# A fused transformer block and graph attention: another assignment and order of the steps on the engines

## The reference, cut to what matters

```python
cmod = silu(c) @ w_ada + b_ada            # six parts of 128
x_mod = ln(x) * (1 + scale_msa) + shift_msa
k, q, v = split(x_mod @ w_qkv, 3)
w = softmax((q / 8) @ k^T)                # per sequence and head, 32 x 32
x = x + gate_msa * ((w @ v) @ w_proj + b_proj)
h = gelu((ln(x) * (1 + scale_mlp) + shift_mlp) @ w_mlp1 + b_mlp1)
x = x + gate_mlp * (h @ w_mlp2 + b_mlp2)
# layer 1: v = x, q = c
self = concat(v, where(sum(v) == 0, 0, q)) @ W_self^T + b_self
for d in (0, 1):                          # adj or its transpose, [:, :, :20]
    aff = (self @ Wq[d]^T + bq) @ (self[:, :20] @ Wk[d]^T + bk)^T / sqrt(8)
    aff = where(sum(A) > 0, aff, -9e15) + (A @ w_bias + b_bias)
    output += (softmax(aff) @ self[:, :20]) @ Wout[d] + bout[d]
return v + relu(self + output)
```

## Time and profile before

| | |
|---|---|
| median of 3 runs | 96.94 us (96.56 to 97.03) |
| the profiled execution | 95.63 us, its span 93.8 us |
| TensorE busy | 83.7 us, 89% of the span |
| VectorE busy | 71.7 us, 76% |
| ScalarE busy | 55.7 us, 59% |
| GpSimd busy | 46.1 us, 49% |
| SyncE's DMA queue | 5.31 MB in 3,496 packets |

### The profile page before, as it was taken

How to read it: one execution, slowest core, us unless ns; L and a number is a source line. 1 busy time by engine, 2 the same in 40 slices (tenths; PEclk the granted TensorE clock), 3 DMA queues, 4 the chain that set the end, 5 groups by cost and what they waited for, 6 DMA issues and landing times.

```text
span 93.8 us, 4196 instructions
## 1 busy us (share of the span) xinstructions
PE 83.7 (89%) x1802; PEld 67.5 (72%) x1802; DVE 71.7 (76%) x183; ACT 55.7 (59%) x127; POOL 46.1 (49%) x72
## 2 busy tenths in 40 slices
...
DMA packets 3778, 5.75 MB, mean 61 GB/s; under 512 B 720, under 2 KB 2896, under 8 KB 3632
## 3 DMA queue, kind: packets, MB, share of 16 engines
q1 hardware_dynamic: 3496, 5.31, 20.6%
...
...
## 4 chain that ended last, share of the span: by engine, by line
PE 65%; DVE 15%; issue 6%; POOL 5%; ACTq 4%; ACT 2%; POOLq 0%; DVEq 0%
PE ps_s L1043 8%; PE ps_b L964 8%; PE ps_b L944 7%; PE ps_b L919 6%; PE ps_b L895 5%; PE ps_b L1069 5%; ACTq L752 4%; PE ps_b L1061 4%; PE ps_b L970 4%; PE ps_b L1091 3%; PE ps_b L912 3%; POOL E L676 3%; DVE neg_max L1445 3%; PE ps_b L1100 2%; PE ps_b L952 2%
## 5 line engine op out<-in xcount | busy, mean ns | idle before, releaser
L1227 ACT ACTIVATE PT<-ps_b 120x384 f32<-120x384 f32 x16 | 7.4, 487 | 8.6 <-PE ps_b L1061 4.6
L1141 ACT ACTIVATE hidden<-ps_b,cols 128x256 f32<-128x256 f32 x16 | 7.0, 474 | 6.5 <-PE ps_b L964 6.5
L856 POOL TENSOR_TENSOR rstd<-var_eps,minus_half 128x2 f32<-128x2 f32 (+1 forms) x9 | 6.0, 668 | 6.3 <-DVE var_eps L1261 6.2
L784 POOL TENSOR_TENSOR Kb<-k_raw,head_mask 128x640 f32<-128x640 f32 x4 | 5.0, 1258 | 8.1 <-ACT k_raw L1156 5.4
L1436 DVE TENSOR_TENSOR E<-ps_s,bias_rep 128x640 f32<-128x640 f32 x8 | 6.6, 823 | 3.0 <-PE ps_b L1061 1.7
L964 PE MATMUL ps_b<-xm,w_rest_sb 128*128 128x256 f32 x32 | 8.6, 385 | 0.0
L676 POOL TENSOR_TENSOR E<-E,neg_max 128x640 f32<-128x640 f32 x5 | 6.4, 1271 | 4.4 <-DVE neg_max L1445 3.9
L1043 PE MATMUL ps_s<-Kb,home_b 32*32 32x80 f32 x512 | 7.4, 239 | 0.7 <-DVE E L1436 0.7
L970 PE MATMUL ps_b<-hidden,w_rest_sb 128*128 128x256 f32 x32 | 7.6, 386 | 0.0
L647 POOL TENSOR_TENSOR xm<-xm,cmod 128x256 f32<-128x256 f32 (+1 forms) x6 | 3.5, 586 | 8.3 <-DVE xm L1283 8.3
L1043 PEld LDWEIGHTS ps_s<-Kb,home_b 32*32 32x32 f32 x512 | 5.7, 103 | 2.4 <-issue 1.5
(11 more groups left out here) (120 smaller groups left out, 218.0 us busy)
## 6 DMA issues: line engine op xcount, KB each, us to landing
...
```

Source lines behind the costliest of these rows:

```text
L856: ins = pool.tensor_tensor(rstd[:, layer, g0:g1], var_eps[:, layer, g0:g1], minus_half[:, 0:g1 - g0], ALU.pow)
L1141: return act.activation(hidden[:, slot_of(h), j, 0:n], ps[:, 0:n], ACT.Gelu_apprx_tanh, bias=cols[:, R_MLP1 + j:R_MLP1 + j + 1])
L1227: ins = act.activation(PT[0:KR, key % 3, 0:CH, :], ps[0:KR, 0:CH * P].rearrange("p (j t) -> p j t", t=P), ACT.Exp)
```

## The change

Nothing of the arithmetic changes: the list has the same 480 steps. FILL goes from 14 products of ones to 5. In ON and TAKE_ON 55 steps change their engine. ORDER and BANKS are another permutation and another choice of banks. The parts that the text below speaks of:

- The products of ones: 12 ahead of k 0 and 2 ahead of xnT 2 before; now 2 ahead of the transpose xnT 0, 1 ahead of q 0, 2 ahead of k 2.
- Start: shift 0 goes to GpSimd, the eviction of q 0 and zero vz1a to ScalarE, the spread of k 0 to GpSimd.
- Steps with two SBUF operands change between VectorE and GpSimd (resid1, resid2, shift, sub, ya, yb, spreads of k1).
- Scores of the two units of a group stand next to each other in TensorE's list before. Now other steps stand between scores 14 and 15, 16 and 17, 18 and 19, and 21 and 20, and in layer 0 between 6 and 7.
- Part 1 of V 1's spread of mid 3 moves from ScalarE's queue to SyncE's, behind part 0 and ahead of the first store. The product v1 of mid 3 stands ahead of scores 17 (behind scores 16).
- Layer 1's first scores, 9 and 8, stand behind more products of mids 1 to 3.

```diff
--- before.py
+++ after.py
@@ -62,7 +62,7 @@
 ZERO_K = (0, 0)
 ZERO_V = (0, 0)
 WARM = 5
-FILL = {('k', 0): 12, ('xnT', 2): 2}
+FILL = {('xnT', 0): 2, ('q', 0): 1, ('k', 2): 2}
...
+ ('resid1', 0): 'dve',
  ('resid1', 2): 'dve',
+ ('resid1', 3): 'dve',
  ('resid2', 0): 'dve',
- ('resid2', 3): 'dve',
- ('shift', (0, 0)): 'dve',
+ ('shift', (0, 0)): 'pool',
  ('shift', (1, 0)): 'dve',
- ('shift', (1, 1)): 'dve',
- ('spread', ('k', 0)): 'act',
+ ('shift', (1, 2)): 'dve',
+ ('shift', (1, 3)): 'dve',
+ ('spread', ('k', 0)): 'pool',
  ('spread', ('k', 1)): 'act',
- ('spread', ('k', 2)): 'act',
- ('spread', ('k', 3)): 'pool',
- ('spread', ('k', 4)): 'act',
+ ('spread', ('k', 2)): 'pool',
+ ('spread', ('k', 3)): 'act',
+ ('spread', ('k', 4)): 'pool',
  ('spread', ('k1', 0, 0)): 'dve',
  ('spread', ('k1', 0, 1)): 'pool',
- ('spread', ('k1', 1, 0)): 'act',
- ('spread', ('k1', 1, 1)): 'pool',
- ('spread', ('k1', 2, 0)): 'act',
- ('spread', ('k1', 2, 1)): 'pool',
- ('spread', ('k1', 3, 0)): 'pool',
- ('spread', ('k1', 3, 1)): 'act',
+ ('spread', ('k1', 1, 0)): 'dve',
+ ('spread', ('k1', 1, 1)): 'act',
+ ('spread', ('k1', 2, 0)): 'dve',
+ ('spread', ('k1', 2, 1)): 'act',
+ ('spread', ('k1', 3, 0)): 'act',
+ ('spread', ('k1', 3, 1)): 'dve',
  ('spread', ('v', 0)): 'act',
- ('spread', ('v', 1)): 'pool',
- ('spread', ('v', 2)): 'act',
- ('spread', ('v', 3)): 'act',
- ('spread', ('v', 4)): 'pool',
- ('spread', ('v1', 3, 1)): 'act',
+ ('spread', ('v', 1)): 'act',
+ ('spread', ('v', 2)): 'pool',
+ ('spread', ('v', 3)): 'pool',
+ ('spread', ('v', 4)): 'act',
+ ('spread', ('v1', 3, 1)): 'sp',
  ('sub', 5): 'dve',
- ('sub', 6): 'dve',
- ('sub', 7): 'pool',
+ ('sub', 6): 'pool',
+ ('sub', 7): 'dve',
  ('sub', 8): 'pool',
  ('sub', 9): 'pool',
  ('sub', 10): 'pool',
  ('sub', 11): 'pool',
- ('sub', 12): 'dve',
+ ('sub', 12): 'pool',
+ ('ya', 2): 'dve',
+ ('ya', 3): 'dve',
+ ('ya', 4): 'dve',
  ('ya', 6): 'dve',
  ('ya', 7): 'dve',
- ('yb', 0): 'dve',
- ('yb', 2): 'dve',
+ ('yb', 1): 'dve',
+ ('yb', 5): 'dve',
+ ('yb', 6): 'dve',
  ('yb', 7): 'dve',
+ ('zero', 'vz1a'): 'act',
...
- (('k', 3), 0): 'dve',
- (('k', 4), 0): 'dve',
- (('k1', 0, 0), 0): 'dve',
  (('k1', 0, 1), 0): 'dve',
  (('k1', 1, 0), 0): 'dve',
- (('k1', 2, 0), 0): 'dve',
- (('k1', 2, 1), 0): 'dve',
- (('q', 0), 0): 'dve',
  (('q', 1), 0): 'dve',
- (('q', 3), 0): 'dve',
- (('sbtok', 0), 0): 'dve',
- (('sbtok', 1), 0): 'dve',
- (('x2tok', 1), 0): 'dve',
- (('x2tok', 2), 0): 'dve',
- (('yT', 0), 0): 'dve',
- (('yT', 1), 0): 'dve'}
+ (('q', 2), 0): 'dve',
+ (('q1', 0, 0), 0): 'dve',
+ (('q1', 0, 1), 0): 'dve',
+ (('q1', 1, 0), 0): 'dve',
+ (('q1', 2, 0), 0): 'dve',
+ (('q1', 2, 1), 0): 'dve',
+ (('sbtok', 3), 0): 'dve',
+ (('yT', 2), 0): 'dve'}
...
-ORDER = [('zero', 'v1_ones'), ('consts', 0), ('zero', 'v0_ones'), ('zero', 'pad'), ('ident', 0), ('masks', 0), ('plus1', 0),
- ('zero', 'vz1a'), ('apply', 0), ('dense', ('xnT', 0)), ('take', (('cmod', 0), 0)), ('take', (('xnT', 0), 0)),
- ('zero', 'vz1b'), ('stats', (0, 1)), ('stats', (0, 2)), ('shift', (0, 0)), ('stats', (0, 3)), ('dense', ('k', 0)),
- ('dense', ('q', 0)), ('fetch', 0), ('rstd', (0, 1)), ('dense', ('v', 0)), ('dense', ('cmod', 1)), ('fetch', 2),
- ('rstd', (0, 2)), ('take', (('q', 0), 0)), ('apply', 1), ('fetch', 1), ('take', (('k', 0), 0)),
...
- ('take', (('xn2T', 3), 0)), ('scores', 9), ('take', (('rowsum', 1), 0)), ('scores', 8), ('shift', (1, 3)),
...
- ('exp', 17), ('scores', 20), ('spread', ('v1', 3, 0)), ('spread', ('v1', 3, 1)), ('turn', 16), ('addx', 2),
- ('badd', 11), ('turn', 19), ('ya', 3), ('turn', 18), ('selfb', 3), ('max', 11), ('scores', 22), ('scores', 23),
...
+ORDER = [('zero', 'v0_ones'), ('ident', 0), ('zero', 'v1_ones'), ('masks', 0), ('consts', 0), ('zero', 'pad'), ('silu', 0),
+ ('plus1', 0), ('sel', 0), ('gbias', 0), ('zero', 'vz1a'), ('dense', ('cmod', 0)), ('stats', (0, 0)),
+ ('take', (('cmod', 0), 0)), ('rstd', (0, 0)), ('apply', 0), ('dense', ('xnT', 0)), ('take', (('xnT', 0), 0)),
+ ('stats', (0, 1)), ('shift', (0, 0)), ('zero', 'vz1b'), ('stats', (0, 2)), ('dense', ('q', 0)), ('rstd', (0, 1)),
+ ('dense', ('k', 0)), ('apply', 1), ('dense', ('v', 0)), ('rstd', (0, 2)), ('stats', (0, 4)), ('dense', ('xnT', 1)),
...
+ ('spread', ('k1', 1, 0)), ('dense', ('k1', 2, 1)), ('scores', 9), ('scores', 8), ('take', (('v1', 1, 0), 0)),
...
+ ('scores', 14), ('max', 7), ('values', 10), ('values', 8), ('take', (('self', 3), 0)), ('scores', 15), ('exp', 11),
+ ('sub', 7), ('dense', ('q1', 3, 1)), ('dense', ('k1', 3, 0)), ('badd', 8), ('take', (('q1', 3, 1), 0)),
+ ('values', 9), ('take', (('k1', 3, 0), 0)), ('values', 11), ('recip', 5), ('scores', 16), ('spread', ('k1', 3, 0)),
+ ('spread', ('v1', 2, 0)), ('max', 8), ('turn', 13), ('dense', ('v1', 3, 0)), ('mult', 5), ('sub', 8), ('recip', 6),
+ ('exp', 13), ('scores', 17), ('take', (('v1', 3, 0), 0)), ('dense', ('k1', 3, 1)), ('mult', 6), ('turn', 12),
...
+ ('selfb', 1), ('take', (('sbtok', 0), 0)), ('scores', 18), ('take', (('x2tok', 0), 0)), ('values', 12), ('yb', 1),
+ ('values', 14), ('max', 9), ('yb', 0), ('relu', 1), ('values', 13), ('exp', 15), ('addx', 1), ('scores', 19),
+ ('relu', 0), ('recip', 7), ('sub', 9), ('values', 15), ('badd', 10), ('dense', ('sbtok', 1)),
+ ('spread', ('v1', 3, 0)), ('dense', ('q1', 3, 0)), ('mult', 7), ('take', (('sbtok', 1), 0)), ('addx', 0),
+ ('scores', 21), ('max', 10), ('take', (('q1', 3, 0), 0)), ('turn', 17), ('selfb', 2), ('turn', 16), ('ya', 2),
+ ('exp', 17), ('sub', 10), ('recip', 8), ('dense', ('sbtok', 2)), ('mult', 8), ('exp', 16), ('scores', 20),
+ ('take', (('sbtok', 2), 0)), ('dense', ('x2tok', 2)), ('spread', ('v1', 3, 1)), ('badd', 11),
+ ('dense', ('x2tok', 1)), ('selfb', 3), ('take', (('x2tok', 2), 0)), ('turn', 18), ('take', (('x2tok', 1), 0)),
...
+ ('addx', 2), ('turn', 21), ('recip', 9), ('store', (2, 4)), ('exp', 20), ('sub', 12), ('values', 19), ('mult', 9),
+ ('exp', 21), ('values', 20), ('recip', 10), ('mult', 10), ('values', 21), ('ya', 4), ('turn', 22), ('recip', 11),
+ ('ya', 5), ('turn', 23), ('mult', 11), ('exp', 22), ('yb', 4), ('exp', 23), ('ya', 6), ('values', 22), ('yb', 5),
...
```

More of the change, by code:

```diff
@@ L166 @@
+ (('q1', 1, 0), 0): 'dve',
[3 more added lines that the diff above has]
+ (('yT', 2), 0): 'dve'}
 BANKS = {('cmod', 0): 0,
- ('xnT', 0): 1,
+ ('xnT', 0): 0,
+ ('q', 0): 0,
  ('k', 0): 1,
- ('q', 0): 0,
  ('v', 0): 2,
- ('cmod', 1): 3,
- ('xnT', 1): 0,
+ ('xnT', 1): 3,
  ('xnT', 2): 3,
- ('xnT', 3): 0,
- ('k', 1): 3,
- ('q', 1): 2,
- 'qz': 1,
+ ('cmod', 1): 2,
+ ('k', 1): 1,
+ ('q', 1): 0,
  ('v', 1): 3,
- ('k', 2): 1,
+ ('xnT', 4): 1,
+ 'qz': 3,
+ ('k', 2): 0,
@@ L180 @@
+ ('xnT', 3): 3,
  ('q', 2): 2,
- ('turn', 0): 1,
- ('xnT', 4): 0,
- ('v', 2): 2,
- ('v', 3): 3,
- ('turn', 1): 2,
- ('k', 3): 0,
- ('q', 3): 3,
- ('q', 4): 1,
- ('values', 0): 0,
- ('v', 4): 2,
+ ('turn', 0): 3,
+ ('v', 3): 0,
+ ('k', 3): 1,
+ ('q', 3): 2,
+ ('v', 2): 0,
+ ('values', 0): 2,
+ ('q', 4): 1,
+ ('turn', 1): 0,
+ ('k', 4): 3,
+ ('v', 4): 1,
+ ('yT', 0): 2,
+ ('turn', 3): 1,
  ('turn', 2): 3,
- ('k', 4): 2,
- ('yT', 0): 0,
- ('turn', 3): 0,
- ('proj', 0): 1,
+ ('proj', 0): 2,
  ('values', 1): 3,
- ('bias', 0): 2,
+ ('turn', 5): 2,
@@ L198 @@
  ('x1tok', 0): 1,
  ('turn', 4): 3,
- ('turn', 5): 0,
- ('values', 2): 0,
- ('values', 3): 3,
+ ('bias', 0): 0,
+ ('values', 2): 3,
+ ('values', 3): 2,
  ('xn2T', 0): 1,
- ('turn', 6): 3,
+ ('turn', 7): 3,
+ ('yT', 1): 2,
+ ('turn', 6): 1,
  ('yT', 2): 0,
- ('turn', 7): 1,
- ('yT', 1): 2,
  ('mlp1', 0, 0): 3,
+ ('proj', 1): 2,
  ('proj', 2): 0,
- ('proj', 1): 1,
- ('mlp1', 0, 2): 2,
- ('mlp1', 0, 3): 0,
- ('mlp1', 0, 1): 1,
+ ('mlp1', 0, 2): 1,
+ ('mlp1', 0, 3): 2,
+ ('mlp1', 0, 1): 0,
  ('x1tok', 2): 3,
- ('values', 4): 2,
@@ L216 @@
[L216 to L218 removed]
+ ('values', 4): 1,
+ ('x1tok', 1): 2,
+ ('mlp2', 0): 0,
+ ('yT', 3): 1,
  ('xn2T', 2): 3,
[L220 to L237 removed]
+ ('xn2T', 1): 2,
@@ L238 @@
+ ('proj', 3): 1,
+ ('rowsum', 0): 0,
+ ('self', 0): 3,
+ ('mlp1', 2, 2): 2,
+ ('mlp1', 2, 0): 0,
+ ('mlp1', 1, 2): 1,
+ ('q1', 0, 0): 2,
+ ('k1', 0, 0): 0,
+ ('k1', 0, 1): 3,
+ ('mlp1', 1, 1): 1,
+ ('v1', 0, 0): 2,
+ ('mlp1', 2, 1): 3,
+ ('mlp1', 1, 3): 1,
+ ('x1tok', 3): 0,
+ ('mlp1', 1, 0): 2,
+ ('q1', 0, 1): 3,
  ('mlp1', 2, 3): 1,
- ('v1', 0, 0): 3,
  ('mlp2', 1): 2,
- ('mlp2', 2): 3,
- ('self', 1): 2,
- ('x2tok', 1): 0,
- ('xn2T', 3): 1,
- ('rowsum', 1): 3,
- ('x2tok', 2): 1,
- ('rowsum', 2): 3,
```

269 lines of the change are left out of this document (122 added, 147 removed), and 7 rows, old and new, of the table ORDER.

## The result

The changed kernel took 98.34 us (median of 20 runs, 96.82 to 99.84), the kernel before beside it 96.44 (20 runs, 95.41 to 97.80). The ratio is 1.016, 95% interval 1.012 to 1.021: slower by 1.6%, where 1.8% faster was forecast. The profiled execution took 97.89 (span 96.2) against 95.63 (span 93.8) before.

The account below looks back on a forecast made before the run. TensorE and VectorE were nearly full, leaving about 3 us of holes plus waste at the start and behind the last product. Terms -0.8 -0.2 -0.5 -0.4 +0.4 -0.2 = -1.7 us take the median 96.94 to 95.2; range 93.4 to 97.4.

Parts of the forecast that it names:

- The start: Up to the first subtraction: fewer products of ones let real products start sooner, gaining 0.8 us, bounds 0 and 1.8.
- The term for xnT 0: First transpose at the start: two products of ones ahead of it cost 0.65 us, making it some 0.3 us later.
- The clock: TensorE at the start: 1.2 GHz until activity releases 2.4 GHz; fewer ones leave no long early run to release it.
- rival B: Start: clock stays at 1.2 GHz to about 17, products take 1.7 us more, gain gone, 97.0; chance 0.14.
- beyond 15: Sign at the start: TensorE products at low pace beyond 15 us would show the forecast wrong.
- The middle: From 17 to 56 us: same work in nearly the same order, gain 0.2 us, bounds 0 and 0.6.
- Two-operand steps: Layer 1, VectorE beside GpSimd: keeping these steps apart gains 0.5 of 1.7 us of waiting, bounds 0 and 1.6.
- The last spread: V 1's last spread, moved to SyncE's queue: ends exp 16's wait on issue, gain 0.4 us, bounds 0 and 1.1.
- The warning that values 20 might wait for the transfers: Near the end: values 20 waiting for V 1's last spread, needed at about 85, was named a sign of being wrong.
- Layer 1: Layer 1's attention: VectorE starts near 57.8 with 22.7 us of work; tighter hand-offs cost 0.4 us, bounds -0.3 and +3.
- rival A: Layer 1 binds through VectorE's idle time: 6.2 us instead of 3.6 makes 97.8 us; chance 0.11.
- Behind the last product: Kernel's end: sums on VectorE and an earlier reciprocal 11 gain 0.2 us, bounds -0.5 and 0.5.

Follow-up runs that it names:

- e3: The changed kernel with the constants, the tile of ones among them, made first on GpSimd; ratio to the kernel before 1.010 (0.998 to 1.022).
- e1: The kernel before with the changed kernel's few products of ones (2 ahead of xnT 0, 1 of K 0, 2 of K 2); ratio 1.001 (0.995 to 1.007).
- e9: The kernel before with the tile of ones made late on GpSimd, as in the changed kernel; ratio 0.995 (0.988 to 1.001).
- e2: The changed kernel with 12 products of ones ahead of q 0 instead of 1; ratio to the kernel before 1.021 (1.004 to 1.037).
- e8: The changed kernel with the last spread of V 1 back on ScalarE's queue; ratio to the kernel before 1.030 (1.024 to 1.037).
- e4: The changed kernel with constants made first on GpSimd and 12 products of ones ahead of q 0; ratio to the kernel before 1.004 (0.997 to 1.011).
- e14: The kernel before with the changed engines for layer 1's 16 two-operand steps alone; ratio 0.996 (0.990 to 1.001).
- e12: The kernel before with the changed engines for all 18 moved two-operand steps, nothing else; ratio 0.989 (0.978 to 0.9996).
- e13: The changed kernel with the 18 two-operand steps back on their old engines; ratio to the kernel before 1.007 (0.997 to 1.018).
- e10: The kernel before with the last spread of V 1 on SyncE's queue instead of ScalarE's; ratio 1.013 (1.006 to 1.020).
- e18: The changed kernel with no products of ones ahead of xnT 0 and six ahead of q 0; ratio to the kernel before 0.988 (0.976 to 0.999).

## Why the prediction was wrong, point by point

**The start (-0.8).** The step that failed. q 0 was over at 8.88, not near 7, and the first subtraction at 17.22, beyond the 16.4 I had named as the sign. The term for xnT 0 was "some 0.3 us later"; it was 1.34. With an early tile it would have held (e3, 0.26). I had missed two moves: the tile of ones 0.9 us later on GpSimd, and the eviction of cmod 0 ahead of apply 0 on VectorE. I also had the two ones ahead of xnT 0 start at 5.0 and cost 0.65; they started at 5.71, and the transpose followed 1.01 us behind their start. e1 (ones ahead of xnT 0, early tile: 5.83) and e9 (late tile, no ones ahead of it: 5.71) show that either alone could have been borne in the old order. My lower bound (0) excluded a loss without a reason.

**The clock (rival B, 0.14).** Its mechanism came true, and further: low until 19.16, where I had said "beyond 15" would be wrong, with scores 1 over at 19.84. But it was not the cause by itself (e1 1.001, e2 1.021), only a part: e8 has the same start as the changed kernel, the full clock 2.4 us sooner and values 7 1.1 us earlier. It was a mistake to take VectorE as what is late: with products at half pace cmod 1 takes 1.75 us, and VectorE waited 0.51 us for it and 0.72 for the next product.

**The middle (-0.2).** From scores 1 to values 7 the changed kernel gained 0.4, where I had forecast 0.2. With the start put right (e4, scores 1 within 0.1 of before) it lost 0.7. A hole on issue inside bias 1 is 0.42 of that; whether the rest comes from bias 1, which now stands behind values 3 to 5, was not tried.

**Two-operand steps (-0.5, bounds 0 and 1.6).** Right in mechanism and near in size where it can be seen alone: 0.7 to 0.9 us by badd 9 and 1.3 to 1.5 by badd 12 in e14 and e12, where I took 0.5. In the changed kernel no sum, subtraction or spread of VectorE is over 0.83 in layer 1's attention (0.8 was stated), but its order gained little by it (e13).

**The last spread (-0.4).** The wait of exp 16 on issue is gone and values 16 are over 0.2 us earlier, in spite of badd 12 being 0.8 later. What I had not looked for took its place 25 instructions on, the 1.45 us of instruction supply. The warning that values 20 might wait for the transfers came true in the old order (e10), not in the new.

**Layer 1 (+0.4, rival A).** It went as in the sum: from the first adding step at 60.96 to the last maximum at 86.34, 25.38 us, VectorE busy 22.39 of them (22.7 said), idle 3.0 (3.6 said).

```profile
60.96:86.34 25.38, 24.04 (x757) 19.13 (x756) 22.39 (x40) 16.04 (x41) 12.86 (x18) 1.00 0.12 26
```

The last maximum is 2.2 us after the 84.1 of the forecast because the stretch began at 60.96 and not at 57.8. That is the start again: from values 7 to the first adding step it is 2.8 us more than before (19.3 against 16.5), where 2.7 was said. Adding steps waited 1.8 us in all for scores, 0.96 once, where I had allowed 0.5; it did not decide.

**Behind the last product (-0.2, bounds -0.5 and 0.5).** From the last maximum to the span's end it was 8.3 before and 9.8 now: +1.5. The term itself was about right: e4, with one hole of 0.65 us there and the full clock to its last product, takes 8.0. What came on top are the holes of the instruction supply and, in the changed kernel's profile, the fallen clock (87.43 to 90.84). e3 and e18 have no fallen clock there, two holes each (1.65 and 0.70, 1.40 and 1.37), and take 9.6 and 10.3. The sum had no term for either hole or clock, nor has any row of before one to size it by.

In all: start and middle +2.1, layer 1 -1.3 up to badd 12, tail +1.6, in the profiled executions; forecast -1.0, -0.5 and -0.2. Of the +2.1 some 0.8 is which executions happened to be profiled, by the means given under the table.
